# A deformable-attention block on one core: the softmax chain one step later, its widened copy on GpSimd

## What is computed

```python
xn = bn(x)
q = grouped_conv1x1(xn, qw)                        # 8 groups of 16 channels
off = tanh(pw(gelu(depthwise_conv(q)))) * 4        # 64 sampling points per group
k, v = gconv(grid_sample(xn, grid + off))          # keys and values at those points
pos = grid_q - grid_kv                             # 1024 queries x 64 keys x 2
bias = sign(pos) * log1p(abs(pos))
bias = relu(bias @ cpb_w1 + cpb_b1)                # hidden 32
bias = relu(bias @ cpb_w2 + cpb_b2)                # hidden 32
sim = q @ k.T * scale + (bias @ cpb_w3 + cpb_b3)   # 8 heads, 1024 x 64
out = softmax(sim) @ v
x = x + project(out) + out_b
x = x + mlp_w2 @ gelu(mlp_w1 @ bn(x) + mlp_b1) + mlp_b2
```

## Time and profile before

| What | Value |
|---|---|
| Runs | 893.63, 896.69, 896.90 us; median 896.69 |
| The profiled execution's own time | 898.17 us |
| Its span, first to last instruction | 896.4 us |
| PE (matmul) busy | 811.4 us, 91% |
| DVE busy | 717.5 us, 80% |
| ACT busy | 676.1 us, 75% |
| GpSimd (POOL) busy | 3.1 us |
| Mean granted TensorE clock | 0.981 of full speed |

### The profile page before, as it was taken

One profiled execution on the slowest core, in us unless ns is written; L12 is line 12 of the kernel. 1 busy time (PEld: TensorE's weight loads), 2 busy tenths in 40 slices (PEclk: granted clock), 3 DMA queues, 4 the chain that ended last, 5 costly groups with the idle time before them and its releaser, 6 DMA issues.

```text
span 896.4 us, 27521 instructions
## 1 busy us (share of the span) xinstructions
PE 811.4 (91%) x12470; PEld 232.1 (26%) x12470; DVE 717.5 (80%) x530; ACT 676.1 (75%) x775; POOL 3.1 (0%) x7
## 2 busy tenths in 40 slices
PE   2299998889999999888999999988999999999997
PEld 1122222222222222222222222222222222222224
DVE  4789799798877589898885869979888668989843
ACT  2468778978777688896776877797878678888863
POOL 1000000000000000000000000000000000000000
PEclk8599999999999999999999999999999999999999
DMA  4502010020110201002020200102002020200000
GB/s 163 120 2 49 3 39 12 12 65 3 43 34 1 48 3 49 12 14 54 1 63 15 49 1 14 37 12 56 12 3 61 14 48 2 72 3 3 2 15 24
DMA packets 18264, 27.67 MB, mean 31 GB/s; under 512 B 10980, under 2 KB 11620, under 8 KB 18148
## 3 DMA queue, kind: packets, MB, share of 16 engines
q1 hardware_dynamic: 18148, 25.91, 11.7%
HBM read 23.05 MB, written 2.74 MB: 29 GB/s over the span
## 4 chain that ended last, share of the span: by engine, by line
PE 67%; ACT 15%; DVE 8%; issue 7%; DMA 2%; SPq 1%; ACTq 0%
PE pair L870 23%; PE scores L888 22%; ACT h L467 8%; PE pair L844 6%; DVE h L621 4%; PE pair L1023 3%; PE scores L899 3%; PE pair L978 2%; PE pair L996 2%; PE pair L1014 2%; DVE big L725 2%; PE scores L984 1%; PE pair L923 1%; ACT big L569 1%; ACT L569 1%
## 5 line engine op out<-in xcount | busy, mean ns | idle before, releaser
L621 DVE TENSOR_TENSOR h<-hxy 128x2048 f32<-128x2048 f32 x256 | 578.1, 2287 | 77.2 <-PE pair L870 73.2
L467 ACT ACTIVATE h<-pair 128x1024 f32<-128x1024 f32 x512 | 517.6, 1024 | 143.4 <-PE pair L844 104.6
L870 PE MATMUL pair<-h,wts 32*32 32x512 f32 x8192 | 299.9, 603 | 19.5 <-ACT h L467 5.5
L888 PE MATMUL scores<-h,wts 128*32 128x512 f32 x2048 | 275.6, 607 | 0.1
L844 PE MATMUL pair<-fy,u_rows 32*128 32x512 bf16 x1024 | 102.8, 387 | 15.3 <-DMA fy<-fy_dram 15.3
L870 PEld LDWEIGHTS pair<-h,wts 32*32 32x32 f32 x8192 | 65.9, 103 | 81.2 <-ACT h L467 35.1
L844 PEld LDWEIGHTS pair<-fy,u_rows 32*128 32x128 bf16 x1024 | 26.5, 91 | 232.6 <-issue 232.6
L888 PEld LDWEIGHTS scores<-h,wts 128*32 128x32 f32 x2048 | 42.1, 108 | 157.3 <-issue 148.2
L748 DVE TENSOR_REDUCE neg_max<-pair 128x8 f32<-128x512 f32 x32 | 22.1, 691 | 22.8 <-PE pair L978 22.8
L978 PE MATMUL pair<-const,probs 128*128 128x128 f32 x128 | 20.5, 284 | 21.6 <-ACT h L467 20.8
L477 ACT ACTIVATE probs<-scores,wts 128x512 f32<-128x512 f32 x32 | 22.0, 688 | 23.7 <-PE scores L888 23.5
(11 more groups left out here) (99 smaller groups left out, 341.3 us busy)
## 6 DMA issues: line engine op xcount, KB each, us to landing
hxy<-features_dram SPq DMA_DIRECT2D x64, 256.0 KB, 4.9
wts<-weights_dram SPq DMA_DIRECT2D x2, 960.0 KB, 7.9
att_den<-reciprocals_dram SPq DMA_DIRECT2D x7, 256.0 KB
x<-x_dram SPq DMA_DIRECT2D x2, 512.0 KB, 5.5
fy<-fy_dram SPq DMA_DIRECT2D x16, 64.0 KB
fy_dram<-fy_part SPq DMA_DIRECT2D x24, 32.0 KB, 3.7
out_dram<-x SPq DMA_DIRECT2D x3, 256.0 KB, 5.4
features_dram<-pos_sign SPq DMA_DIRECT2D x4, 128.0 KB, 2.3
```

Source lines behind the costliest of these rows:

```text
L467: emptied("z", 2 * g + j, act.activation(h2[j][g % H2_BUFS][:].rearrange("p r n -> p (r n)"), pair_of("z", 2 * g + j)[:], ACT.Relu))
L621: dve.tensor_tensor(h1[g % H1_BUFS][:].rearrange("p c (y x) -> p c y x", x=W), hx[unit % 2][:, :, t].unsqueeze(2).broadcast_to([128, CT, H ...
L870: ins = pe.matmul(z_of(g, r)[32 * c:32 * (c + 1)], w(l, "w2")[key_rows(r), key_rows(r)], h1[g % H1_BUFS][key_rows(r), c], start=r >= 2, st ...
L888: ins = pe.matmul(scores[phase % 2][32 * r:32 * (r + 1)], w(l, "w3")[:, 32 * t:32 * (t + 1)], h2[rows[0] // 2][step % H2_BUFS][:, r % 2], ...
```

## The change

It moves every stage of the softmax chain, and every stage of the end of a half (AFTER_SLOTS), one step later; offset with offset_tanh and keys_values with keys_values_out move one step later too, and fy_weights of layer 1 one step. copy_scores stays. widen_max goes from ACT's list to a list of GpSimd's own, one step before max_off as before, and is a tensor_copy there with the same waits.

```diff
-    ("dve", "conv_sum", 1): 34, ("act", "conv_gelu", 0): 33, ("pe", "offset", 0): 35,
-    ("act", "offset_tanh", 0): 35, ("dve", "positions", 0): 38, ("pe", "spread", 0): 37,
+    ("dve", "conv_sum", 1): 34, ("act", "conv_gelu", 0): 33, ("pe", "offset", 0): 36,
+    ("act", "offset_tanh", 0): 36, ("dve", "positions", 0): 38, ("pe", "spread", 0): 37,
...
-    ("pe", "keys_values", 0): 51, ("act", "keys_values_out", 0): 51,
+    ("pe", "keys_values", 0): 52, ("act", "keys_values_out", 0): 52,
 }
 AFTER_SLOTS = {
-    ("pe", "attend", 0): 5, ("act", "attend_out", 0): 5, ("dve", "reciprocal", 0): 9, ("dve", "divide", 0): 12,
-    ("pe", "project", 0): 12, ("dve", "residual1", 0): 14, ("pe", "mlp_up", 0): 14, ("act", "mlp_gelu", 0): 14,
-    ("pe", "mlp_up", 1): 15, ("act", "mlp_gelu", 1): 15, ("pe", "mlp_down", 0): 17, ("dve", "residual2", 0): 19,
+    ("pe", "attend", 0): 6, ("act", "attend_out", 0): 6, ("dve", "reciprocal", 0): 10, ("dve", "divide", 0): 13,
+    ("pe", "project", 0): 13, ("dve", "residual1", 0): 15, ("pe", "mlp_up", 0): 15, ("act", "mlp_gelu", 0): 15,
+    ("pe", "mlp_up", 1): 16, ("act", "mlp_gelu", 1): 16, ("pe", "mlp_down", 0): 18, ("dve", "residual2", 0): 20,
 }
-SOFTMAX_SLOTS = {("pe", "scores_t"): 2, ("dve", "score_max"): 4, ("act", "widen_max"): 3,
-                 ("pe", "max_off"): 4, ("act", "exp"): 4}
+SOFTMAX_SLOTS = {("pe", "scores_t"): 3, ("dve", "score_max"): 5, ("pool", "widen_max"): 4,
+                 ("pe", "max_off"): 5, ("act", "exp"): 5}
...
-    put("dve", 21, "fy_weights", 1)
+    put("dve", 22, "fy_weights", 1)
...
         @block.gpsimd
         def _(pool):
+            def widen_max(phase):
+
+                wait_emptied(pool, "scores_t", phase)
+                if phase:
+                    pool.wait_ge(max_taken_off, phase)
+                pool.tensor_copy(neg_max_wide[:], neg_max[phase % 2][:].unsqueeze(2).broadcast_to([128, CHUNKS, NKV]))\
+                    .then_inc(max_widened, 1)
+
+            stages = {"widen_max": widen_max}
             for p in range(2):
                 pool.memset(qpad[p][:], 0.0).then_inc(borders_zeroed, 1)
             pool.memset(fy[0][:], 1.0).then_inc(ones_set, 1)
+            for g in range(LAST_STEP + 1):
+                for name, n in PLAN["pool"].get(g, []):
+                    stages[name](n)
...
-            def widen_max(phase):
-
-
-                wait_emptied(act, "scores_t", phase)
-                if phase:
-                    act.wait_ge(max_taken_off, phase)
-                act.activation(neg_max_wide[:], neg_max[phase % 2][:].unsqueeze(2).broadcast_to([128, CHUNKS, NKV]), ACT.Copy)\
-                    .then_inc(max_widened, 1)
```

More of the change, by code:

```diff
@@ L124, in plan @@
 def plan():
-    at = {e: {} for e in ("pe", "act", "dve")}
+    at = {e: {} for e in ("pe", "act", "dve", "pool")}
     parts = {}
@@ L580, in _ @@
                       "distances": distances, "attend_out": attend_out,
-                      "keys_values_out": keys_values_out, "exp": exp, "widen_max": widen_max,
+                      "keys_values_out": keys_values_out, "exp": exp,
                       "mlp_gelu": mlp_gelu}
```

## The result

The changed kernel takes 940.06 us (median of four runs, 938.51 to 942.09), the kernel before, run beside it, 896.80. The ratio is 1.048, with a 95% interval of 1.046 to 1.050: slower by 43 us. The forecast was 890.7, 880 to 903. The profiled execution took 938.51 us with a span of 936.7.

The account below looks back on a forecast made before the run. PE was taken to set the pace (67% of the chain), with its idle time to be won. 9.3 us gained less 3.3 given back left 6.0 net: 892.2 like for like, 890.7 against the median, range 880 to 903.

Parts of the forecast that it names:

- The step that failed: GpSimd's widened copy before max_off: some 4.0 us free, copy taken as 0.8, so PE loses 0.
- The second rival: max_off on PE waits for a late widened copy, 1.4 us in 31 phases, about 934 us; chance 0.13.
- the memset's price: GpSimd's copy of 512 elements, priced from a 1156-element memset of 1.06 us: 0.47 to 1.06, taken as 0.8.
- within 0.3 us: Steps 41 to 48: hidden_terms runs ahead of score_max, yet DVE's run reaches layer 2 of step 48 this close to before.
- scores_t's start: Quiet phases: scores_t starts 1.27 us behind layer 2 instead of 1.55, its step 3.15 instead of 3.43; 4.5 us in all.
- the wait at L978: PE idle before scores_t, put down to ACT's relu: 20.8 us in 31 phases, to fall under 5 us.
- Widening off ACT: Before keys_values, whose step now lacks the copy on ACT: 0.5 us in each of three, 1.5 gained.
- The tail: End of the kernel, no matrix work to hide anything: 0.6 from the later attend plus 0.3 from GpSimd, 0.9 us lost.
- The MLP's two steps: Ends of halves: the first mlp_up shares its step with queries-by-keys; two steps take 0.4 us less, 2.4 in six halves.
- A copy between two operations: DVE's loss to GpSimd's copy, up to its whole length: booked in steps 44 to 49 as 3 x 0.8 = 2.4 us.
- 6.0 net: Whole kernel: 9.3 us gained less 3.3 given back.
- Steps 33 to 50: Three segments with the long scores_t stalls, 11.1 us: nothing booked, as later waits at layer 2 stay within 0.3 us.

Follow-up runs that it names:

- e4: The changed kernel with GpSimd's copy replaced by a fill with zeros of the same size, place and waits; 896.87 us, ratio 1.000.
- e1: The changed kernel's moved steps with the widened copy left on ACT, one step before max_off; 899.89 us, ratio 1.001 to the kernel before.
- e10: The changed kernel with hidden_terms behind score_max and spread, features and spread_out one step later (37 to 38); 891.43 us, ratio 0.994.
- e7: The changed kernel with hidden_terms one step later too (12 to 13), behind score_max on DVE again; 898.77 us, ratio 1.003.
- e18: The changed kernel with VectorE waiting for its own two operations of the terms right behind them; 899.99 us, ratio 1.002.
- e11: The changed kernel with the widened copy left on ScalarE and spread, features and the copy behind them one step later (38); 894.46 us, ratio 0.998.
- e16: The changed kernel with each operation of the terms written with two inputs instead of one, still at step 12; 974.12 us, ratio 1.087.
- e2: The kernel before, its steps kept, with only the widened copy moved to GpSimd; 897.26 us, ratio 1.000.
- e8: The kernel before, its steps kept, with the widened copy on GpSimd and four h1 buffers instead of three; 896.31 us, ratio 0.998.
- e12: The changed kernel with the first layer's terms at step 14 of 16 instead of 12; 899.35 us, ratio 1.003.
- e14: The changed kernel with one more wait of VectorE, for its own first-layer operations so far, ahead of the reduce; 898.62 us, ratio 1.0036.
- e17: The changed kernel with the terms behind the reduce (step 15) and two unneeded larger-of-two operations in their place at step 12; 904.84 us, ratio 1.009.
- e3: The changed kernel with DVE waiting after score_max until the widened copy is done; 901.04 us, ratio 1.005.

## Why the prediction was wrong

**The step that failed** is "Even behind one DVE operation of 2.29 it ends in 3.1 to 3.4. PE pays 0 by this". Alone the copy takes 0.61 us (0.8 was taken), and behind one operation it ends in 2.61, so the price was even high. But in 12 phases it stood behind a run of two first-layer operations, of three, or of three and eight smaller ones (4.81, 7.01, 9.97 us), and in eight of them the time until max_off was not enough. The second rival had the place, the price and the point: max_off waiting, about 934, above 4.0 us. Its count was off (1.4 us in 31 phases; measured 3.3 to 4.5 in eight, and over half as much again by the clock), so it is luck that its 934 lies near 940. It got 0.13.

**What spoke against it** was the rule of the Trainium skill's page "SBUF — State Buffer", section "Who interferes with whom": whoever issues first has the shared ports for its whole instruction. The trace agrees for the 16 copies of 2.61 us in the changed kernel, and for the 28 fills of e4 beside first-layer operations, which only write and were not held. For copies of 4.81 to 9.97 us behind a run of instructions it does not hold as I used it: it does not say whose turn comes next when further instructions of VectorE stand ready, and that it is the other side's I read in. Without that reading the rival had only the memset's price against it, and deserved more than 0.13.

**What I saw and did not follow.** The text says that hidden_terms now runs ahead of score_max, and prices it by DVE's time alone, within 0.3 us. That was right for DVE and missed what it does to GpSimd.

**What held.** scores_t's start, forecast 1.27 us behind layer 2, is 1.28, its step 3.16 (3.15), the wait at L978, now L981, 3.2 (under 5). Widening off ACT gives 1.5 us at keys_values: the wait of layer 2 there is 2.8 in e1 and 1.3 in the changed kernel. The tail loses 0.5 us from the start of the last layer 2 to the end of the span (896.4 - 865.78 = 30.6 to 936.7 - 905.63 = 31.1; 0.9 booked). The MLP's two steps take 500.33 - 495.07 = 5.26 and 504.91 - 500.33 = 4.58 us, 0.19 less than before instead of 0.4, so 1.1 us in six halves and not 2.4. A copy between two operations cost DVE 0.41 and not 0.8. PE's idle time without the waits for GpSimd fell by 9.7 us, but this is not a gain of 9.7: e10, which keeps the moved steps and has neither loss, has 12.3 less idle time and PE busy for 5.3 more, and is 5.5 us faster than the kernel before by the medians. 6.0 net was forecast.

**Steps 33 to 50, booked at nothing.** In waiting, that was near: of the 2.05 us at scores_t 0.58 and 0.52 come back at the corrections and layer 2, of the 1.65 there 1.07 stays, and layer 2 of step 38 waits 2.9 in place of 1.1 and 1.0. But one wait of 2.9 is not two of 1 us: in some executions the clock falls behind it. This second error explains most of why e1, e7 and e18 bring nothing although PE waits 7 to 9 us less. It is shown for e7 by e10; for e1, e11 points the same way, and for e18 it is inferred.

## What to carry to other kernels

Before a small operation goes to GpSimd, list for each place what VectorE has run since its last pause, not only what runs beside it; if VectorE must keep its order, one wait for its own last operation can be enough. When steps move, look at which stages of the other engines change places with them, and try first to keep the old neighbours together (e7 does so with one number). And price a wait on TensorE by what follows it too: merging two short waits into one long one can lower the clock and give back all that the steps saved.

## What the runs showed of the hardware

**A reading GpSimd operation can be held over several VectorE instructions.** In the 12 profiles with the copy beside a first-layer operation there are 288 copies that start beside one. Sorted after the runs by one rule, they part almost cleanly: has an operation with per-partition scalars (the terms or the norm, in either form) started before the end of a two-input operation ahead of it, and has each operation since started before the end of the one ahead (by 0.08 us)? Where not, 237 of 237 copies are 2.6 us. Where so, 48 of 51 are 4.8 to 10.0; the three others (e16) have a next first-layer operation that starts 0.03 to 0.08 us late, itself a pause. (Without the words on the two-input operation ahead, two more copies, in e2 and e8, are exceptions.) How long a copy is held depends on the length of VectorE's run: all 48 end 0.47 to 0.48 us behind one of its operations, and behind these VectorE stood still, in 32 cases for 4.9 us or more, in nine for 0.47; behind the other seven a convolution product or the terms followed without a pause. That the terms' place and a pause decide is shown by e7, e12, e14 and e18, that neither lateness nor the fast form does by e17 and e16; the rule as a whole was found by sorting and not tried by itself, and what in the chip keeps GpSimd out stays open.

**A wait of 2.9 us can lower the clock, and need not.** In the profiles of e3, e4, e7 and e12 the matmuls behind all three waits ran at the lower level, in e14 behind none, in e18 behind two of three and in the changed kernel behind one. What decides it is not shown.
